# Fixed expert tiles: each 64-row half multiplied in its own half of the array's columns

## What is computed

```python
logits_fk = einsum('bsd,nd->bsn', x @ W_fk + b_fk, emb_fk_n)      # and logits_rk with W_rk, emb_rk_n
w_fk, _ = topk_sparsify(softmax(logits_fk), 4)                    # 4 of 128 weights kept, renormalised
w_rk, _ = topk_sparsify(softmax(logits_rk), 4)
h   = einsum('bsnr,bsn->bsr', einsum('bsd,ndr->bsnr', x, f_know), w_fk)
out = einsum('bsnd,bsn->bsd', einsum('bsr,nrd->bsnd', h, r_know), w_rk)
```

## Time and profile before

| | us |
|---|---|
| timed runs before, median of 3 | 1009.42 (1008.91 to 1011.6) |
| span of the profiled execution, first to last instruction | 1005.3 |
| what lies around the span (median less span) | 4.1 |
| first product, PE's first to last matmul | about 560 to 778 |
| second product, part 0 | about 785 to 866 |
| second product, part 1 | about 875 to 953 |
| rest (last fetches, sums, stores) | about 953 to 1005 |

### The profile page before, as it was taken

How to read it: one execution, slowest core, us unless ns; L and a number is a source line. 1 busy time by engine, 2 the same in 40 slices (tenths; PEclk the granted TensorE clock), 3 DMA queues, 4 the chain that set the end, 5 groups by cost and what they waited for, 6 DMA issues and landing times.

```text
span 1005.3 us, 21117 instructions
## 1 busy us (share of the span) xinstructions
PE 842.1 (84%) x5575; PEld 692.3 (69%) x5575; DVE 691.8 (69%) x4357; ACT 431.6 (43%) x1339; POOL 552.8 (55%) x764
## 2 busy tenths in 40 slices
PE   5789999999999999977731799999999799699900
PEld 3778888888888777754420688999988458565800
DVE  2199999999999899947694599874444244255423
ACT  0134334434444344425430254444544488578800
POOL 5256556665666565525477471007773677673065
PEclk9689989989999599967555799999999799899955
DMA  9233443443433265201732876557898677588533
GB/s 319 96 136 125 171 170 136 148 145 140 169 115 118 103 205 184 89 21 34 183 104 75 260 244 174 140 154 204 283 408 335 210 261 254 191 276 283 191 106 90
DMA packets 81580, 177.17 MB, mean 176 GB/s; under 512 B 12952, under 2 KB 38232, under 8 KB 78648
## 3 DMA queue, kind: packets, MB, share of 16 engines
q1 hardware_dynamic: 56088, 120.62, 37.2%
q10 hardware_dynamic: 14112, 32.12, 8.3%
q0 software_dynamic: 11264, 23.09, 7.7%
HBM read 94.25 MB, written 81.53 MB: 175 GB/s over the span
## 4 chain that ended last, share of the span: by engine, by line
PE 31%; DVE 28%; POOL 17%; issue 13%; ACT 6%; DMA 3%; SPq 1%; ACTq 1%; POOLq 0%; DVEq 0%
PE bank L1198 17%; DVE work L1335 12%; DVE top L1329 9%; ACT m_y L926 5%; POOL early L742 5%; PE bank L1186 4%; POOL slots_g L749 3%; POOL slots_x L720 3%; PE bank L1243 2%; PE bank L954 1%; PE bank L974 1%; POOL eqbd L622 1%; PE bank L999 1%; DMA early<-in_vocab,ids 1%; POOL sc L672 1%
## 5 line engine op out<-in xcount | busy, mean ns | idle before, releaser
L1335 DVE MATCH_REPLACE8 work<-top,work 128x68 f32<-128x68 f32 x896 | 179.2, 211 | 0.1
L906 ACT ACTIVATE m_y<-bank 64x128 f32<-64x128 f32 x392 | 106.3, 271 | 144.9 <-PE bank L1198 142.6
L926 ACT ACTIVATE m_y<-bank 64x192 f32<-64x192 f32 x392 | 127.1, 324 | 49.7 <-PE bank L1243 27.0
L1198 PE MATMUL bank<-f_all,place 96*128 (+1 forms) x792 | 146.3, 329 | 0.0
L1329 DVE MAX8 top<-work 128x8 f32<-128x68 f32 x896 | 128.9, 213 | 6.5 <-ACT tru L792 6.2
L1198 PEld LDWEIGHTS bank<-f_all,place 96*128 96x128 f32 x792 | 117.4, 193 | 7.4 <-issue 0.2
L1243 PE MATMUL bank<-r_all,place 128*128 (+1 forms) x396 | 118.2, 423 | 0.2 <-ACT m_y L926 0.2
L742 POOL DMA_INDIRECT early<-slots_h,s_all x68 | 65.6, 964 | 89.2 <-DMA slots_h<-m_y 68.8
L1604 DVE COPY place<-bank 96x256 f32<-96x256 f32 x147 | 57.4, 417 | 81.5 <-PE bank L1186 77.1
L1612 DVE COPY place<-bank 128x128 f32<-128x128 f32 x147 | 38.0, 287 | 100.8 <-PE bank L1234 100.6
L954 PE MATMUL bank<-early,xp 128*128 128x192 f32 x432 | 94.2, 382 | 6.7 <-DMA xp<-in_a_x 5.2
(11 more groups left out here) (187 smaller groups left out, 1692.9 us busy)
## 6 DMA issues: line engine op xcount, KB each, us to landing
early<-slots_x SPq DMA_DIRECT2D x49, 384.0 KB, 3.9
slots_y<-m_y ACTq DMA_DIRECT2D x49, 384.0 KB, 3.2
slots_h<-m_y ACTq DMA_DIRECT2D x49, 256.0 KB, 4.4
early<-slots_g SPq DMA_DIRECT2D x49, 256.0 KB, 3.3
f_all<-in_f_know SPq DMA_DIRECT2D x16, 768.0 KB, 9.3
r_all<-in_r_know SPq DMA_DIRECT2D x16, 768.0 KB
slots_x<-zero SPq DMA_DIRECT2D x28, 360.0 KB, 3.0
slots_x<-zero SPq DMA_DIRECT2D x28, 336.0 KB, 3.3
```

Source lines behind the costliest of these rows:

```text
L906: last = nc.scalar.activation(m_yh[rows, d, t, :], bank[2 + t][rows, h * R:(h + 1) * R], ACT.Copy)
L926: last = nc.scalar.activation(m_y[rows, d, t, :], bank[2 + t][rows, h * D:(h + 1) * D], ACT.Copy)
L1198: last = nc.tensor.matmul(into, m_xT[t][0:HALF, c, :], matrix[:, ..., c * R:(c + 1) * R], start=(c == 0), stop=(c == 1))
L1335: last = nc.vector.match_replace(work[:, par, c, :], top8[:, c, :], work[:, par, c, :], TAKEN)
```

## The change

In fixed tiles, each half of 64 rows is multiplied with its own expert's matrix alone. The stationary operand of a matmul is cut to the 64 columns of that half, and its output goes to that half's 64 partitions of PSUM, that is, to the lower or upper half of the array's columns. In the first product the order of the four matmuls of a tile becomes step 0 half 0, step 0 half 1, step 1 half 0, step 1 half 1; in the second product half 0, half 1. Both halves write the same columns of the bank (0 to 127, or 0 to 191), so one eviction of 128 partitions replaces the two of 64. Spill tiles stay as they are (`own` is false): two full-width products, two evictions. Nothing else changes: transposes, copies, DMAs, waits and the order of the groups are the same.

```diff
-                    for h in range(2):
-                        rows = slice(h * HALVED, (h + 1) * HALVED)
-                        last = nc.scalar.activation(m_yh[rows, d, t, :], bank[2 + t][rows, h * R:(h + 1) * R], ACT.Copy)
+                    if first_order(g)[n] < PART_MAIN:
+                        last = nc.scalar.activation(m_yh[:, d, t, :], bank[2 + t][:, 0:R], ACT.Copy)
+                    else:
+                        for h in range(2):
+                            rows = slice(h * HALVED, (h + 1) * HALVED)
+                            last = nc.scalar.activation(m_yh[rows, d, t, :], bank[2 + t][rows, h * R:(h + 1) * R], ACT.Copy)
...
-            def multiply_first(j, t, pair):
+            def multiply_first(j, t, pair, own):
...
-                n = R * (2 // len(pair))
-                for h, matrix in enumerate(pair):
-                    into = bank[2 + t][:, h * n:(h + 1) * n]
-                    for c in range(2):
-                        last = nc.tensor.matmul(into, m_xT[t][0:HALF, c, :], matrix[:, ..., c * R:(c + 1) * R], start=(c == 0), stop=(c == 1))
+                for c, h in ((0, 0), (0, 1), (1, 0), (1, 1)) if own else ((0, 0), (1, 0), (0, 1), (1, 1)):
+                    rows = slice(h * HALVED, (h + 1) * HALVED)
+                    into, stays = (bank[2 + t][rows, 0:R], rows) if own else (bank[2 + t][:, h * R:(h + 1) * R], slice(0, P))
+                    last = nc.tensor.matmul(into, m_xT[t][0:HALF, c, stays], pair[h][:, c * R:(c + 1) * R], start=(c == 0), stop=(c == 1))
...
-                n = D * (2 // len(pair))
                 for h, matrix in enumerate(pair):
-                    last = nc.tensor.matmul(bank[2 + t][:, h * n:(h + 1) * n], m_xT[t][:, 0, :], matrix, start=True, stop=True)
+                    rows = slice(h * HALVED, (h + 1) * HALVED)
+                    into, stays = (bank[2 + t][rows, 0:D], rows) if own else (bank[2 + t][:, h * D:(h + 1) * D], slice(0, P))
+                    last = nc.tensor.matmul(into, m_xT[t][:, 0, stays], matrix, start=True, stop=True)
...
-                        pairs = [[r_all[:, e:e + 2, :].rearrange("p e d -> p (e d)")] for e in at]
+                        pairs = [[r_all[:, e + h, :] for h in range(2)] for e in at]
```

More of the change, by code:

```diff
@@ L923, in keep_second @@
                     act.wait_ge(sem["m_mm1"], j * GROUP + t + 1)
-                    for h in range(2):
-                        rows = slice(h * HALVED, (h + 1) * HALVED)
-                        last = nc.scalar.activation(m_y[rows, d, t, :], bank[2 + t][rows, h * D:(h + 1) * D], ACT.Copy)
+                    if j - FIRST_GROUP[g] < PART_MAIN:
+                        last = nc.scalar.activation(m_y[:, d, t, :], bank[2 + t][:, 0:D], ACT.Copy)
+                    else:
+                        for h in range(2):
+                            rows = slice(h * HALVED, (h + 1) * HALVED)
+                            last = nc.scalar.activation(m_y[rows, d, t, :], bank[2 + t][rows, h * D:(h + 1) * D], ACT.Copy)
                     last.then_inc(sem["m_done1"], 1)
@@ L1193, in multiply_first, with first_product @@
                     pe.wait_ge(sem["m_done0"], (j - 1) * GROUP + t + 1)
-                n = R * (2 // len(pair))
-                for h, matrix in enumerate(pair):
-                    into = bank[2 + t][:, h * n:(h + 1) * n]
-                    for c in range(2):
-                        last = nc.tensor.matmul(into, m_xT[t][0:HALF, c, :], matrix[:, ..., c * R:(c + 1) * R], start=(c == 0), stop=(c == 1))
+                for c, h in ((0, 0), (0, 1), (1, 0), (1, 1)) if own else ((0, 0), (1, 0), (0, 1), (1, 1)):
+                    rows = slice(h * HALVED, (h + 1) * HALVED)
+                    into, stays = (bank[2 + t][rows, 0:R], rows) if own else (bank[2 + t][:, h * R:(h + 1) * R], slice(0, P))
+                    last = nc.tensor.matmul(into, m_xT[t][0:HALF, c, stays], pair[h][:, c * R:(c + 1) * R], start=(c == 0), stop=(c == 1))
                 last.then_inc(sem["m_mm0"], 1)
-            def first_product(g, n, pairs):
+            def first_product(g, n, pairs, own):
                 j = FIRST_GROUP[g] + n
@@ L1209, in first_product @@
                     for now in range(t, t + AHEAD):
-                        multiply_first(j, now, pairs[now])
+                        multiply_first(j, now, pairs[now], own)
             pe.wait_ge(sem["tiles_known"], 1)
@@ L1221, in _ @@
                         at = [(jj * GROUP + t) * 2 for t in range(GROUP)]
-                        pairs = [[f_all[0:HALF, e:e + 2, :]] for e in at]
+                        pairs = [[f_all[0:HALF, e + h, :] for h in range(2)] for e in at]
                     else:
@@ L1225, in _ @@
                         pairs = [[f_all[0:HALF, bass.ds(e[2 * t + h], 1), :].squeeze(1) for h in range(2)] for t in range(GROUP)]
-                    first_product(g, n, pairs)
+                    first_product(g, n, pairs, jj < PART_MAIN)
             def turn_second(j, t):
@@ L1234, in turn_second, with multiply_second @@
                 nc.tensor.transpose(turn_bank[t][:, 0:P], m_h[:, d, t, :], ident[:]).then_inc(sem["m_turn1"], 1)
-            def multiply_second(j, t, pair):
+            def multiply_second(j, t, pair, own):
                 pe.wait_ge(sem["m_xt1"], j * GROUP + t + 1)
@@ L1240, in multiply_second, with second_product @@
                     pe.wait_ge(sem["m_done1"], (j - 1) * GROUP + t + 1)
-                n = D * (2 // len(pair))
                 for h, matrix in enumerate(pair):
-                    last = nc.tensor.matmul(bank[2 + t][:, h * n:(h + 1) * n], m_xT[t][:, 0, :], matrix, start=True, stop=True)
+                    rows = slice(h * HALVED, (h + 1) * HALVED)
+                    into, stays = (bank[2 + t][rows, 0:D], rows) if own else (bank[2 + t][:, h * D:(h + 1) * D], slice(0, P))
+                    last = nc.tensor.matmul(into, m_xT[t][:, 0, stays], matrix, start=True, stop=True)
                 last.then_inc(sem["m_mm1"], 1)
-            def second_product(g, j, pairs):
+            def second_product(g, j, pairs, own):
                 stop = FIRST_GROUP[g] + PART_GROUPS[g]
@@ L1254, in second_product @@
                     for now in range(t, t + AHEAD):
-                        multiply_second(j, now, pairs[now])
+                        multiply_second(j, now, pairs[now], own)
             pe.wait_ge(sem["m_done0"], GROUPS * GROUP)
@@ L1268, in _ @@
                         pairs = [[r_all[:, bass.ds(e[2 * t + h], 1), :].squeeze(1) for h in range(2)] for t in range(GROUP)]
-                    second_product(g, FIRST_GROUP[g] + jj, pairs)
+                    second_product(g, FIRST_GROUP[g] + jj, pairs, jj < PART_MAIN)
         @block.vector
```

## The result

The changed kernel takes 984.93 us (median of 4 runs, 982.9 to 990.96) beside 1010.06 for the kernel before: ratio 0.9758, 95% interval 0.9728 to 0.9788, by the ratio some 24 us less. The prediction was 992.5. The profiled execution has a span of 981.1 us, 24.2 less than before.

| stage | before, us | after, us | gain | forecast |
|---|---|---|---|---|
| up to the first product | 559.6 | 560.2 | -0.6 | 0 |
| first product, part 0 fixed | 70.7 | 68.5 | 2.2 | 3.4 |
| spill groups of both parts | 75.9 | 76.6 | -0.7 | 0 |
| part 1 fixed, up to the second product | 79.1 | 75.1 | 4.0 | 5 |
| second product, part 0 and the wait for part 1 | 89.9 | 82.4 | 7.5 | 4.5 |

What follows compares the result with a forecast made beforehand. PE was taken as always busy in four fixed-group stretches, each with another resource nearly full; gains 3.4 + 5 + 4.5 + 4 = 16.9 us off the 1005.3 us span leave 988.4, plus 4.1 gives 992.5 us, range 985 to 1000.

Steps and rivals of the forecast that it cites:

- rival A: Both products on PE: the halves do not stream together, shape changes are paid for nothing; about +37 us, 1046 us; chance 0.16.
- 8 forecast: Sign of a right forecast: the second product begins some 8 us earlier, its part 1 some 13 us earlier.
- (C): Rival: PE's gain is swallowed by DMA and DVE's sums, only part 0's 3.4 us is sure; 1006 us; chance 0.07.
- (D): Rival: PE, with gaps in part 0, is granted the lower clock, 7.3 us a group there; about +48 us; chance 0.03.
- The slots on PE: Overlapped records per half-group: 9 slots, 0.97 us, taken as 1.09 for issue (first product); 5 slots, 0.81 us (second).
- The change of shape: Between full-width transposes and half-width matmuls on PE: a pair of changes costs 0.21 to 0.32 us, taken as 0.30.
- The estimate of 1.6 to 1.7x: Speedup of two column tiles on PE, from the skill's 2.38x for three; would make the 1.73 us about 1.05.
- Second product, part 1: Fixed groups: same PE gain as part 0, with DMA at 0.94 and outputs between DVE's copies; 4 us, bounds 2 and 6.
- Second product, part 0: 16 fixed groups: PE gains 5.8 to 8.2 us, capped by POOL's transfers and its 4.43 us wait; 4.5 us taken.
- First product, part 0: 16 fixed groups: DVE's 4.13 us a group cuts off PE's 3.66, leaving 0.21 a group; 3.4 us.
- First product, part 1: 16 fixed groups: PE alone would gain 10.9 us, full DMA engines would leave 1.3; 5 us taken.
- What had been put at 0: Stretches forecast to gain nothing: up to the first product, the spill groups, and the rest after the fixed groups.

Runs made afterwards that it cites:

- run 4: Changed kernel with both halves multiplied one after the other in the same first 64 columns of the array, two evictions a tile: 1046.8 us, ratio 1.0373.
- run 3: Changed kernel with two evictions of 64 partitions per fixed tile again in place of one of 128, in both products: 1004.47 us, ratio 0.9962.
- run 10: Changed kernel with AHEAD = 4 in place of 2: four tiles turned, then four multiplied, one pair of shape changes a group: 989.93 us, ratio 0.9805.
- run 11: Changed kernel with AHEAD = 1: one tile turned, then one multiplied, four pairs of shape changes a group: 1138.37 us, ratio 1.1266.
- run 7: Changed kernel with the last 6 of the 16 loads of r_all issued behind the last row loads of part 1: 983.46 us, ratio 0.9745.
- run 9: Changed kernel with all 16 loads of r_all issued behind the last row load of part 1: 996.13 us, ratio 0.9865.
- run 1: Changed kernel with the second product's fixed tiles put back as before, so the change is in the first product alone: 1004.29 us, ratio 0.9964.
- run 5: Changed kernel with the first product's fixed tiles multiplied left, left, right, right in place of left, right, left, right: 988.02 us, ratio 0.978.
- run 6: Changed kernel with the first four fixed groups of the first product's part 0 full-width, with two evictions: 987.08 us, ratio 0.9766.
- run 8: Changed kernel with the edits of run 6 and run 7 together: 986.78 us, ratio 0.9763.
- run 2: Changed kernel with the first product's fixed tiles put back as before, so the change is in the second product alone: 993.38 us, ratio 0.984.
- run 12: Changed kernel with AHEAD = 1 and the first four fixed groups of the first product's part 0 full-width: 1136.43 us, ratio 1.1254.

## Why the prediction was right, and where it was off

The direction and the cause were right: the halves overlap (run 4 without it: 1046.8 us, rival A's own price), and the merged eviction is what lets the second product have the gain (run 3). The gain in the span was 24.2 us in place of 16.9, because some terms of the sum were mis-sized; 984.93 us lies 0.07 past the fast edge of the range 985 to 1000. That the total came so near is in part luck: the terms were off in opposite directions. The three stretches of the first product gained 5.5 us in place of 8.4, the two of the second 18.1 in place of 8.5.

Not all signs were those of the forecast. The second product began 4.9 us earlier (8 forecast), its part 1 12.4 (13). Two signs that the prediction had called wrong also came up: gaps of PE with DVE's copies as releaser (C) and a granted clock under 0.9, 0.89 in both windows of the first product (D). Neither decided the time, as the parts below show.

**The slots on PE** (step "with overlap the first and the last record of a run stand alone": 9 and 5 slots). They do not stand alone. In the trace the records start in pairs, 6 to 7 ns apart, from the first on, a pair every 0.109 us in the first product and every 0.162 in the second: 8 and 4 slots. In the second product that is one slot of 0.16 us per half-group, 0.32 per group, 5.1 us in 16 groups. In the first product the step had even put 1.09 us for issue; it is 0.88, which is worth little there, since DVE and the row loads hold PE up.

The change of shape was priced at 0.30 and costs 0.32 us a pair, the upper of the two bounds, by run 4, by run 10 (one pair less a group, 0.32 less) and by run 11 (two more, 0.66 more). The Trainium skill, "TensorEngine Tiling (Array Packing)", Key Properties, says that a switch of the tiling mode drains the engine and that tiles load and multiply independently. The price of 0.32 us fits the first, though no run here shows the drain itself; the 0.88 us for 16 records show the second. The Trainium skill, "TensorE: Matmul & The Clock Gate", Part 3, The mechanism, on which rival A leaned, lets loads overlap running matmuls only where row groups differ; here both halves use the same 96 rows, and 16 loads and 16 matmuls take the time of 8 streams, so the measurement decides against it. The estimate of 1.6 to 1.7x that the prediction made from the Trainium skill's "TensorE: Matmul & The Clock Gate", Measured speedup vs the span model, was low: 1.74 to 0.88 us is 2.0x.

**Second product, part 1: 4 forecast, 10.6 measured.** Against ACT's 3.17 PE gained not 0.51 but 0.83 us a group (2.34), 13.3 in 16. I had then cut the gain by half, for DMA "already at 0.94" and "the outputs between DVE's copies". In fact 2.7 was lost: 2.0 in five groups in which PE waits for DVE's copies (2.72 to 2.84 us each) and 0.7 in the first two, which start at the low clock. A window of before read 0.94 and 309 GB/s; at the same time of the span, which now holds later groups, it reads:

```profile
886.00:896.00 10.00, 9.66 (x84) 5.57 (x84) 5.67 (x22) 5.24 (x17) 7.56 (x9) 1.00 1.03 382
```

Here the busy share was no measure of the room left; the bytes were a better one. The highest rate in the rows of before was 373 GB/s, a fifth above 309, and 5 us of the same trace (766 to 771) reach 418.

**Second product, part 0: 4.5 forecast, 7.5 measured.** The mechanism was right (PE gained 12.5 us in its fixed groups and then waited 6.5 longer for POOL), the cap was read too low. I took POOL's last wait, 4.43 us, for all its slack. The waits of POOL for a sum over the stretch 781 to 870 of the kernel before (us in total, times, longest), and over 776 to 863 of the changed one:

```profile
POOL slots_g L749 <- DVE early L1632: 8.2, 2, 4.4
...
POOL slots_g L749 <- DVE early L1638: 0.7, 1, 0.7
```

There were two waits, 8.2 us together; afterwards 0.7 is left, and the 7.5 between is what the stretch gained. POOL's slack is used up, and by its waits it is now the bound of that stretch; no run made POOL faster to show it.

**First product, part 0: 3.4 forecast, 2.2 measured.** DVE does cap PE at 4.12 us a group, 0.01 from the forecast; PE waits for copies (PE's waits over 562 to 628: us in total, times, longest):

```profile
PE bank L1203 <- DVE place L1610: 9.3, 12, 0.9
```

What was missing is the slow start at 1.2 GHz, 3.5 us by run 7. Without it the gain would have been 5.7 (70.7 less run 7's 65.0), above the forecast: the first groups run ahead of DVE's cap there (3.36 to 3.84 us), and the kernel before had a short slow start of its own (5.14 and 4.90 us for its first two groups in place of 4.34). So 3.4 and 2.2 are near each other by two omissions of opposite sign. Rival D had the clock in it, but at 48 us and with the wrong trigger: from 576 on PE has gaps (42.69 of 52 us) and the clock is full, and where it was low PE was marked busy all the time.

**First product, part 1: 5 forecast, 4.0 measured.** Right in kind and size: beside the loads of the matrices PE's gain of 1.06 us a group turns into pauses for rows (run 9 has none without them) and the low clock behind the pauses.

**What had been put at 0.** The -0.6 is within what the start of the products moves from run to run (560 to 566 us). The -0.7 is not noise: the first spill group takes 5.07 us in place of 4.39, with PE waiting 0.86 for DVE's copies, and the spill groups take 76.5 to 76.6 us in all of runs 1, 3 and 5 to 9. The 1.2 us of the rest were not followed up; it is 78.1 to 78.8 us in the runs with the second product changed (runs 2 and 5 to 9) and 79.6 and 79.9 in runs 1 and 3.

None of the variants beats the changed kernel. The two things that by the waits now hold it, the transfers in part 1 of the first product and POOL between the parts of the second, were not reduced by any of them.

## What to carry to other kernels

Where half of the array's output is thrown away, two half-width matmuls in the two halves of its columns cost the time of one, and the order within a tile hardly matters; charge 0.3 us for every pair of changes between full and half width, and merge what evicts them, or the evicting engine takes the gain away. Before a gain is cut by "the DMA is nearly full", compare the bytes per second with the highest rate in the same profile, and before it is cut by another engine's slack, add up all waits of that engine in the stretch and not only the last one. A faster TensorE that pauses for data can lose its clock, so a pause can cost more than its own length: behind the pause of 3.03 us in the changed kernel two groups took 5.87 us in place of 3.28.

## What the runs showed of the hardware

- Halves of the array's columns work side by side with the same rows: 16 records of 128 columns in 0.88 us, 1.74 in the same half (run 4). Across the halves they need not start in the order of the program (run 5).
- A pair of changes between full-width transposes and half-width matmuls costs 0.32 us at full clock (runs 4, 10 and 11).
- An eviction from PSUM costs nearly the same for 64 and 128 partitions: 271 and 278 ns for 128 columns.
- The granted clock did not follow the marked busy time of PE. In narrow groups at the start of part 0 it stood at 0.50 for 15 us with PE busy 15.00 of 15.00, and for as long in runs 1, 3, 5 and 9; in run 7 with the same code it was up after 4, and in run 11 it stayed at 0.50 for 110 us. Under full-width groups it was up some 6 us after the start (run 6; in the kernel before, a window of 566 to 576 reads 1.00 where the changed kernel reads 0.50), and so it was under narrow matmuls that do not overlap (run 4: 0.88 in the window 572 to 574, the first product having begun at 566.3). Narrow groups at full clock lost it behind pauses of 3.03 us (748 in the changed kernel), 2.06 (run 7) and 1.68 (run 12), but not behind one of 1.89 (734 in the changed kernel). The Trainium skill, "TensorE: Matmul & The Clock Gate", Part 1, says that the length of the slow start varies between runs of one kernel, by some half a microsecond; the starts of the changed kernel and of run 7 differ by 11 us, so here that does not account for it. What decides between them was not settled.
